# The softmax denominators without the cleared corner: sum products split into 64 and 192 columns at the first step of each sequence

## What is computed

```python
def _L0_attn_ref(x, Wq, bq, Wk, bk, Wv, bv, Wo, bo):      # x: (8, 1024, 512), 16 heads of 32
    Q = split_heads(x @ Wq.T + bq)                        # K and V alike
    scores = jnp.einsum('bhid,bhjd->bhij', Q, K) / jnp.sqrt(jnp.float32(hd))
    delta = t[:, None] - t[None, :]
    causal_mask = delta < 0
    decay = jnp.where(causal_mask, 0.0, -delta.astype(jnp.float32) ** ALPHA)
    scores = jnp.where(causal_mask, -jnp.inf, scores) + decay
    attn = jax.nn.softmax(scores, axis=-1)
    out = jnp.einsum('bhij,bhjd->bhid', attn, V)
    return out @ Wo.T + bo
...
x = L0_attn_x
x = x + _layernorm(_L0_attn_ref(_layernorm(x, axis=-1), ...), axis=-1)
x = x + _layernorm(_L0_ffn_ref(_layernorm(x, axis=-1), L0_ffn_weight), axis=-1)
```

## Time and profile before

| | |
|---|---|
| median of 3 runs | 1152.51 us (1152.26 to 1153.24) |
| the profiled execution's own time | 1153.24 us |
| its span, first to last instruction | 1151.6 us |
| TensorE matmul busy | 1083.2 us, 94% |
| VectorE busy | 985.4 us, 86% |
| ScalarE, GpSimd busy | 708.0 us, 590 us |
| mean granted TensorE clock | 0.978 |

### The profile page before, as it was taken

One profiled execution on the slowest core, in us unless ns is written; L12 is line 12 of the kernel. 1 busy time (PEld: TensorE's weight loads), 2 busy tenths in 40 slices (PEclk: granted clock), 3 DMA queues, 4 the chain that ended last, 5 costly groups with the idle time before them and its releaser, 6 DMA issues.

```text
span 1151.6 us, 44392 instructions
## 1 busy us (share of the span) xinstructions
PE 1083.2 (94%) x18369; PEld 726.2 (63%) x18400; DVE 985.4 (86%) x2572; ACT 708.0 (61%) x1493; POOL 589.7 (51%) x723
## 2 busy tenths in 40 slices
PE   4899999999999999999999999999999999999852
PEld 3566666676666676676666676666667676667421
DVE  5859998889988888899888889988888998887684
ACT  5455666766576676656666665666676656666542
POOL 1334555555554655555555565555655655465421
PEclk9999999999999999999999999999999999999876
DMA  9647666655566675566667565556765665665311
GB/s 276 140 108 146 142 151 164 144 145 137 139 127 152 163 152 141 140 144 132 145 153 168 126 156 132 132 139 156 166 146 139 139 138 131 154 140 131 93 49 44
DMA packets 204830, 161.78 MB, mean 140 GB/s; under 512 B 150449, under 2 KB 150705, under 8 KB 204529
## 3 DMA queue, kind: packets, MB, share of 16 engines
q1 hardware_dynamic: 199888, 141.86, 55.1%
q0 software_dynamic: 4736, 17.04, 4.2%
HBM read 40.87 MB, written 16.78 MB: 50 GB/s over the span
## 4 chain that ended last, share of the span: by engine, by line
PE 72%; DVE 20%; issue 3%; DMA 2%; ACT 1%; SPq 1%; POOLq 1%; POOL 0%; DVEq 0%; ACTq 0%
PE f_job L1392 47%; PE f_st L1493 6%; PE f_o L1512 5%; PE f_o L1515 3%; PE f_job L1568 3%; DVE f_bst L1028 2%; PE f_job L1468 2%; DVE f_rmax L991 2%; PE f_job L1550 2%; DVE f_stage L977 2%; DVE f_inverse L1020 1%; DVE f_x L1072 1%; PE f_job L1558 1%; DVE f_o L1018 1%; DVE f_z L1130 1%
## 5 line engine op out<-in xcount | busy, mean ns | idle before, releaser
L508 POOL TENSOR_SCALAR_AFFINE_SELECT f_PT<-f_PT 64x512 f32<-64x512 f32 (+1 forms) x256 | 205.3, 819 | 144.3 <-ACT f_PT L674 100.0
L523 POOL TENSOR_TENSOR f_square<-f_stage 128x512 bf16<-128x512 f16 x128 | 130.9, 1045 | 88.1 <-ACT f_stage L652 74.2
L1392 PE MATMUL f_job<-f_xTh,f_wqh 128*128 128x256 f16 x512 | 140.8, 275 | 17.8 <-DMA f_xTl<-f_xl 14.7
L514 POOL TENSOR_TENSOR f_OTl<-f_o,f_OTh 128x256 f16<-128x256 f32 x127 | 84.0, 668 | 135.4 <-ACT f_OTh L692 135.3
L652 ACT ACTIVATE f_stage<-f_job,f_bias 128x256 f16<-128x256 f32 x256 | 106.4, 467 | 74.2 <-PE f_job L1392 66.9
L1392 PE MATMUL f_job<-f_xTl,f_wqh 128*128 128x256 f16 x512 | 140.1, 274 | 0.0
L1392 PE MATMUL f_job<-f_xTh,f_wql 128*128 128x256 f16 x512 | 140.1, 274 | 0.0
L1392 PE MATMUL f_job<-f_xTh,f_wkh 128*128 128x256 f16 x512 | 139.9, 273 | 0.0
L1392 PE MATMUL f_job<-f_xTh,f_wkl 128*128 128x256 f16 x512 | 139.8, 273 | 0.0
L1392 PE MATMUL f_job<-f_xTl,f_wkh 128*128 128x256 f16 x512 | 139.7, 273 | 0.0
L977 DVE SCALAR_TENSOR_TENSOR f_stage<-f_job,f_bias,f_stage 128x256 f16<-128x256 f32 x256 | 111.1, 477 | 29.5 <-ACT f_stage L652 28.9
(11 more groups left out here) (199 smaller groups left out, 2957.0 us busy)
## 6 DMA issues: line engine op xcount, KB each, us to landing
f_stacks<-f_stage SPq DMA_DIRECT2D x380, 128.0 KB
f_xin<-x SPq DMA_DIRECT2D x33, 512.0 KB, 4.0
f_x<-x SPq DMA_DIRECT2D x31, 512.0 KB, 4.6
out<-f_z POOLq DMA_DIRECT2D x31, 512.0 KB, 3.3
f_Vmix<-f_V SPq DMA_DIRECT2D x32, 256.0 KB, 3.3
f_Vmix<-f_V SPq DMA_DIRECT2D x64, 128.0 KB, 3.3
f_stacks<-rows_const SPq DMA_DIRECT2D x3, 512.0 KB, 5.3
f_stacks<-wqT SPq DMA_DIRECT2D x2, 512.0 KB, 6.3
```

What stands on the lines that cost most here:

```text
L508: nc.gpsimd.affine_select(out=d, in_=d, compare_op=ALU.is_ge, fill=0.0, base=odd * SUB, pattern=[[0, 4], [0, TP], [1, SUB]], channel_multi ...
L514: nc.gpsimd.tensor_tensor(OT[s % 2][1][:, g, :], o32[:, g % 2, :], OT[s % 2][0][:, g, :], ALU.subtract).then_inc(OTl_made, 1)
L523: nc.gpsimd.tensor_tensor(square[:, 2 * m + pair, :], h, h, ALU.mult).then_inc(squared, 1)
L1392: mm = pe.matmul(dst, lhs[a](c), rhs[b](c), start=(n == 0), stop=(n == 3 * KC - 1))
```

## The change

The two corners are no longer cleared, and TensorE no longer waits for that. Instead the product with ones reads, at the first step of a sequence, only 64 partitions for the first 64 columns and all 128 for the other 192: 8 products per group where there were 4. At the other steps nothing differs. The numbers that are computed are the same.

```diff
-        past_cleared = sem("past_cleared")
...
-            def clear_past(s, g):
-
-                until(dve, pv_done, 4 * s + g - 1)
-                nc.vector.memset(PT[g % 2][SUB:P, :, 0:SUB], 0.0).then_inc(past_cleared, 1)
...
             split_max(0)
-            clear_past(0, 0)
-            clear_past(0, 1)
...
-                if s and s % PER == 0:
-                    clear_past(s, 1)
                 qk_low_part(n, 1)
...
                 normalise(s, 2)
-                if n % PER == 0:
-                    clear_past(n, 0)
...
-                if s % PER == 0 and g < 2:
-                    pe.wait_ge(past_cleared, 2 * (s // PER) + g + 1)
...
-                for r in range(4):
-                    mm = pe.matmul(dst[r * HD:(r + 1) * HD, W2:D], ones[:], weights[:, r, :], start=True, stop=True)
+                for lo, hi in ((0, W2),) if s % PER else ((0, SUB), (SUB, W2)):
+                    keys, _ = values_of(s, lo // SUB)
+                    for r in range(4):
+                        mm = pe.matmul(dst[r * HD:(r + 1) * HD, W2 + lo:W2 + hi], ones[keys], weights[keys, r, lo:hi],
+                                       start=True, stop=True)
                 mm.then_inc(pv_done, 1)
```

## The result

The changed kernel takes 1160.49 us (median of 4 runs, 1159.83 to 1161.64) where the kernel before took 1152.88 in the same comparison (1152.26 to 1153.76). The ratio is 1.0066, with a 95% interval of 1.0049 to 1.0084: 7.6 us slower, between 5.6 and 9.7. The forecast was 3.9 us slower, at 1156.4, with a range up to 1160.0. The sign was right, the size half of what was measured, and the time lies 0.5 us above the range. The profiled execution took 1160.8 us with a span of 1159.0, which is 7.4 us more than the span of before.

The account below looks back on a forecast made before the run. TensorE, busy 94% of the span, was taken as the bound. Turns -4.0, start -0.8, shape changes +8.1 at full and +0.6 at half clock sum to +3.9 us: from 1152.5 to 1156.4 us, range 1152.0 to 1160.0.

Parts of the forecast that it names:

- The price of a change of shape: In weigh at first steps: two more changes between 64- and 128-partition groups per call, 0.27 us, 8.1 us for 30 calls.
- faster: Rival: the change of shape in weigh costs nothing and the gains stand alone, 1147.7 us; chance 0.07.
- no change: Rival: one of the two shape borders in weigh costs and the other hides, 1152.2 us; chance 0.10.
- more: Rival: the added records in weigh cost a group's 0.11 us more per call, 1159.9 us; chance 0.08.
- The wait at the turns: TensorE's wait for DVE before qk(n, 3) at seven turns between sequences goes whole, 0.58 us each, 4.0 us gained.
- the gain does not come: Rival: without the clears another late input holds qk(n, 3) at the turns as long, 1161.2 us; chance 0.07.
- What is late next at that place is nothing: the lists behind it are those of the ordinary turn, which shows no wait there.: At the seven turns: no new wait replaces the one removed before qk(n, 3), so the 4.0 us gain stays whole.
- DVE, with 1.0 us less to do and TensorE later, has more slack: After weigh at first steps: nothing covers the added cost, and DVE will not hold TensorE up; no further cost counted.
- two calls with two changes make 0.6 us: Step 0's weigh(0, 0) and weigh(0, 1) at half clock: each change of shape costs 0.16 us, 0.6 us in all.
- -0.8 for the clears: Kernel start: without the two clears the L977 pair starts 0.77 us earlier, and qk(1, 3) with it; 0.8 us gained.

Follow-up runs that it names:

- e4: Changed kernel with another order in weigh at first steps: values' chunk 0, then the ones' first 64 columns, then the full-height groups; ratio 0.9978 to the kernel before.
- r4: As e4, but weigh(s, 0) of a first step ends with the small groups and weigh(s, 1) begins with them; 1149.23 us, ratio 0.9976 to the kernel before.
- e1: Kernel before without the clears at the seven turns, product with ones whole, some denominators counting old weights; 1150.85 against 1153.22 us, ratio 0.9978.
- r3: Changed kernel with two neighbours in GpSimd's list exchanged, the variance root ahead of the second subtraction; 1157.79 us, ratio 1.0044 to the kernel before.
- r1: Kernel before run again, no edit, for a second trace; ratio 0.9997.
- e3: The change at steps 4 to 28 only, step 0 as in the kernel before; 1157.68 us, ratio 1.0046.
- t2: Kernel before a third time, no edit; ratio 1.0000.
- r2: Changed kernel run again, no edit; 1160.12 against 1152.19 us for the kernel before, ratio 1.0064.
- s4: Changed kernel a third time, no edit; 1160.92 us in 2 runs, ratio 1.0078 to the kernel before.
- t3: Changed kernel a fourth time, no edit; 1160.50 us, ratio 1.0061 to the kernel before.
- s1: Kernel before with the change at step 0 alone: no clears or waits there, product with ones split; 1156.98 against 1151.64 us, ratio 1.0045.
- e2: Kernel before with only the product with ones split at first steps, clears and waits kept; 1161.72 against 1153.22 us, ratio 1.0071.
- s2: Kernel before with the product with ones split at step 0 only, all clears kept; 1157.97 us, ratio 1.0053.
- t1: Changed kernel with the two 64-partition groups of each weigh call put together in step 0 only; 1159.56 us, ratio 1.0060 to the kernel before.
- s3: r3 and r4 together; 1146.27 against 1151.64 us for the kernel before, ratio 0.9952.

## Why the prediction was half right, step by step

**The price of a change of shape was right.** Forecast 0.27 us per call at full clock, measured 0.28 (2.86 - 2.30 for two calls), 28 x 0.28 = 7.8 us at steps 4 to 28. That the records themselves cost next to nothing is shown by e4, and that a single border costs by the pair in r4, where one border less makes 0.14 us. With this the rivals "faster", "no change" and "more" fall.

**The wait at the turns went as forecast.** 0.58 us at each of seven turns, 4.0 us. The rival "the gain does not come" falls in its form.

**The step that failed first: "What is late next at that place is nothing: the lists behind it are those of the ordinary turn, which shows no wait there."** I had looked for waits of TensorE and not at what DVE does in the ordinary turn. DVE's variance instruction took over 0.8 us in 12 of the 32 steps of the kernel before already, and in none of the seven turns; the delay by the clears had just spared them that meeting. In the changed kernel it is 19 steps, the seven turns among them. Without the clears DVE loses 0.65 us of the 1.0 us that it gained, while TensorE comes 0.58 us earlier. So DVE's pair at L976 ends 0.70 us after the start of the scores where it was 0.48 (320.53 and 319.83; 317.07 and 316.59), and TensorE, which at a first step has 16 records of scores before the output product instead of 20, has no slack for it. The sentence "DVE, with 1.0 us less to do and TensorE later, has more slack" fails with it. Given back are 1.3 us in e1, without any split, and 1.5 us in the changed kernel. r3 removes it by moving GpSimd alone.

The Trainium skill (SBUF — State Buffer, "Who interferes with whom") says that VectorE's second pair of ports is shared with GpSimd as an exclusive lock, that whoever comes second is blocked for the whole instruction, and that `tensor_scalar` is among the operations which can take that pair. The trace agrees in that the instruction took 0.81 us instead of 0.17 and ended with GpSimd's second subtraction. But it was held for longer than the one instruction that had begun before it. The first subtraction runs from 317.25 to 317.92, DVE's instruction starts at 317.76, and the second subtraction starts only at 317.88:

```profile
317.25 0.67 POOL L513 TENSOR_TENSOR f_OTl<-f_o,f_OTh 128x256 f16<-128x256 f32 x1
317.88 0.66 POOL L513 TENSOR_TENSOR f_OTl<-f_o,f_OTh 128x256 f16<-128x256 f32 x1
```

Nor is it held every time: in the kernel before, at 680.73, it began as far into the same two subtractions and took 0.19 us. What decides this no run here shows.

**The step that was sized wrong: step 0, "two calls with two changes make 0.6 us", with nothing for the work behind the calls.** The forecast for step 0 was -0.8 for the clears, +0.6 and +0.5 (two of the 30 calls at full clock), +0.4 in sum. From the first scores matmul of step 0 to the start of `qk(2, 1)` the traces give:

| kernels | us, each trace | mean |
|---|---|---|
| step 0 as before: before, r1, e1, e3, t2 | 36.2, 36.2, 37.2, 36.8, 37.8 | 36.8 |
| step 0 changed: after, r2, s4, t3, r3, s1 | 39.0, 38.9, 38.5, 38.7, 38.0, 38.3 | 38.5 |
| step 0 split, clears kept: e2, s2 | 38.7, 39.5 | 39.1 |
| groups together: e4, r4, t1 | 36.5, 36.6, 36.5 | 36.5 |

So step 0 costs 1.7 us instead of 0.4, 1.3 us more than forecast. The clears gave what was forecast: from the first scores to `qk(1, 3)` pass 5.8 us in before, r1, e1 and e3 and 5.1 to 5.2 us in the six kernels of the second row. The two calls at half clock cost what was forecast, too, when the clock is the same: where the whole pair ran at 1.2 GHz it takes 4.04 us unsplit (e1, t2) and 4.65 to 4.67 us split (after, r2, s2, s4, t3). What was missed is, as far as the traces tell, how much of the work behind lies at half clock. The window from 52 to 72 us of the kernel before and of the changed one (length, busy times, PEclk, DMA share, GB/s):

```profile
52.00:72.00 20.00, 16.86 (x353) 10.05 (x351) 10.13 (x19) 12.64 (x32) 5.92 (x10) 0.91 0.71 159
```

```profile
52.00:72.00 20.00, 17.06 (x287) 9.86 (x287) 8.87 (x17) 12.01 (x30) 5.66 (x9) 0.74 0.71 159
```

The granted clock is 0.91 and 0.74 in the mean, 3.4 and 10.2 us at 1.2 GHz. In both, TensorE had waited 2.5 us for DVE, a wait that ended 1.8 us before the clock fell in the first and 0.6 us before it in the second. s3 had the same wait, and there the clock did not fall. In the kernel before the clock rose again 0.6 us before the end of the pair, which took 3.54 us; in the changed kernel the pair took 4.67, and the product `values(1, 0)` behind it 4.24 us instead of 2.70. I had priced the two calls at half clock as if the stretch ended with them.

Whether the change makes the stretch longer, I tried to settle with further traces of both kinds of step 0, and could not. Unchanged step 0: 3.4, 3.4, 6.8, 6.8 and 10.2 us (in two pieces). Split step 0: 10.2, 10.2, 6.8, 10.2, 6.8, 6.8, 10.2 and 6.8 us. It leans to longer with the split, but t2 has 10.2 us without it. And the length is not all: at 6.8 us step 0 takes 36.8 and 37.2 us unchanged and 38.0 to 38.5 changed, at 10.2 us it takes 37.8 and 38.7 to 39.0, so at equal length 1.0 to 1.3 us remain between the means where 0.4 was forecast. t1, made to shorten it, saved 2.1 us in this part of the trace but only 0.9 us in the time. That step 0 is costlier than forecast is shown by the table; that the place and length of the stretch make it is argued, and how much of it is chance stays open.

**The sum with the measured terms:** 7.8 + 1.7 - 4.0 + 1.5 = 7.0 us against 7.4 between the two first spans and 7.6 in the ratio. The remaining 0.4 to 0.6 us are not assigned; behind step 0 alone the traces of one and the same kernel differ by as much. Forecast 3.9, plus 1.5 for the turns, 1.3 for step 0 and 0.3 for the 0.01 us per call, makes the same 7.0.

From `qk(2, 1)` of step 0 to the end, where step 0 has no part, the three traces of the kernel before take 1074.3 to 1074.9 us and the four of the changed kernel 1079.1 to 1080.4, in the mean 5.2 us more. The terms of steps 4 to 28 make 7.8 - 4.0 + 1.5 = 5.3.

## What to carry to other kernels

A short product of other height between full ones is paid by the two changes of shape around it, 0.13 to 0.14 us each here, and not by its columns; set products of one height side by side and the same split is free. When a delay is taken off an engine, do not stop at the wait that vanishes: follow that engine's own list further and look at what its instructions now meet on a neighbour, since an ordinary step may hold a loss that hides under slack. And try the neighbour's order: here two exchanged calls in GpSimd's list, with the grouped products, turned +7.6 us into -5.5 us, of which the missing half-clock stretch near 60 us may be a part.

## What the runs showed of the hardware that was not expected

- A VectorE instruction over 2 elements per partition took 0.81 us beside two GpSimd subtractions over 256 that followed each other (after, step 8). It took 0.17 us when GpSimd was idle (before), and 0.19 to 0.23 us when it started beside a single such subtraction (r3).
- The same program showed half-clock stretches in its first 70 us of 3.4 us in two traces and of 10.2 us in a third (before, r1, t2). These three executions took 1153.24, 1152.81 and 1153.87 us.
- Two variants (s1, s2) took 3.7 to 4.5 us between their span and their time, in every run, where the others took 1.5 to 2.0. So a comparison of a microsecond or two needs the span beside the time.
